# Front of batch b+2 interleaved with the back part of batch b, first jobs inside direction 3, convolution as diagonal matmuls

## Chip, cores and metric

The kernel runs on one core of a Trainium2 chip. The metric is the device time of one execution in microseconds (us), as the median of several; before the change it is 11132.13 us. The engines are called PE (TensorE), ACT (ScalarE), DVE (VectorE), POOL (GpSimd) and SP (SyncE, which issues all the DMAs here).

## What is computed

The input x is 8 batches of 96 channels on a 48 by 48 image (2304 positions). Two residual blocks follow each other, each behind a group norm (32 groups of 3 channels):

```python
x = x + L0(group_norm(x))        # Mamba-like 2D scan
x = x + L1(group_norm(x))        # channel attention over positions
# L0: 96 -> 2 x 192 channels (xx, z)
xx = gelu(conv3x3_depthwise(xx) + conv_b)            # 192 channels
# four directions k: rows, columns, and both backwards
dts, B, C = split(x_proj[k] @ xs[k])                 # 12, 16, 16 rows
delta = softplus(dt_w[k] @ dts + dt_b[k])            # 192 x 2304
h = h * exp(delta * A) + (delta * u) * B             # 192 channels x 16 states, over 2304 positions
y = sum_n(h * C) + u * D                             # directions summed
out = out_proj @ (layernorm(y) * gelu(z))
# L1: qkv = depthwise conv3x3(w_qkv @ x); 8 heads of 12; q, k normalised
out = w_proj @ softmax(q k^T * scale) v              # 2304 x 2304 scores a head
```

## The kernel before

Each batch passes three parts. The **front** is the group norm, the in-projection, the convolution, the x-projection and the nine first jobs of direction 0. The **directions** are the scans. The **back** is LayerNorm, the gate, the out-projection, the second group norm, the qkv projection and convolution, the norms of q and k, and their splitting in three bf16 parts each. The attention of batch b needs the back of b, and runs inside the directions of batch b+1; that of batch 7 runs alone at the end. `batches` writes this order for every engine: front(0), directions(0), back(0), then a loop over batches 1 to 7 of front, directions (with the attention of the batch before) and back, then attention(7).

**Directions.** There are four, each with 72 steps, written as three *stretches* of 24 steps (`BODY`); the first stretch is written out and the other two are turns of a loop. A step handles 8 channels x 16 states (128 partitions) and 768 positions. PE broadcasts delta*u by a bf16 matmul (`broadcast_u`, L1187 and L1188, in two PSUM slots), DVE multiplies it by B (`mult_b`, L992) and scans (L1013), ACT has taken the exponential of delta*A (L786, ring of six loads, issued five steps ahead), POOL multiplies by C (L691), PE sums the 16 states (`sum_tile`, L1200, bank 6) and DVE takes the sums out (L1020, L1022). B and C lie in `rep`; its thirds for the next direction are loaded as the old ones come free (`load_rep`).

**Jobs.** What a direction needs (delta, and delta*u split in three bf16 parts) is made one direction earlier by three jobs a stretch: a matmul with `dt_proj` (`job`, L1229, L1234), ACT's abs, relu, exp and ln (`job_stage`), POOL's six operations (`job_split`), and SP's stores (`store_delta`, `store_job`). They start at the steps `JOB_START = (1, 6, 13)`. Direction 3 makes none. Direction 0's nine jobs are made in the front, with DVE in POOL's place. The inputs u and dts lie in SBUF for the whole batch.

**Attention** in a step is three score matmuls (L1278), three exponentials on ACT (L795) and the value matmuls (L1212). Scores and jobs share PSUM banks 0 and 1 in turn (`SCAN_RING = 2`); a matmul waits until ACT has read what stood in its bank two entries before. The leftovers of the chunk before come at steps 1 to 4 (copy, denominators, their ln and exp, division), 7 (projection) and 16 (residual).

**The front's convolution** of 128 channels is DVE's (L977, nine operations over 2304 positions); that of 64 channels is ACT products and POOL sums (`front_units`). In the back, DVE convolves q and k (16 operations, L977) while ACT and POOL do v (`back_units`). All engines run their instructions in the order written.

## Time and profile before

| | us |
|---|---|
| median of 3 runs | 11132.13 (11129.79 to 11133.89) |
| profiled execution, its own time | 11130.08 |
| its span, first to last instruction | 11128.2 |
| busy: PE, DVE | 7464.3, 8043.1 |
| busy: ACT, POOL | 6426.9, 6356.7 |
| mean granted clock of PE | 0.786 |

The share of busy time is a mean over stages that differ. A granted clock of 1.0 is PE's 2.4 GHz, 0.5 is 1.2 GHz. A float32 matmul shows as two records. The numbers after L are lines of the kernel before. A row of the windows view has, in this order: the window's start and end and its width in us; busy us and instructions of PE, PE's weight loads, DVE, ACT and POOL; the granted clock; the DMA engines' busy share and their GB/s. A row of the lines view has the busy us of the group, the mean ns of one instruction, and the idle us before it with what ended it.

### The profile page before, as it was taken

To read this page: it belongs to the slowest core of one execution; us is meant where nothing else is said; L and a number is where in the kernel's file an instruction comes from. 1 tells how busy PE (TensorE), PEld (TensorE's weight loads), DVE (VectorE), ACT (ScalarE), POOL (GpSimd) and SP (SyncE) were. 2 spreads that over 40 slices of the span, in tenths; PEclk is the share of its full clock that TensorE was granted. 3 is DMA by queue.
4 is the path that set the end of the run, shared out by engine and by line. 5 is a ranking of instruction groups with operands and counts; after the bars stand their busy time and mean duration, and the time that the engine had idled before them with its cause. 6 is when DMAs were issued, how large, how long until landed. Compare 5 with 4: busy or idle time off the path is not lost.

```text
span 11128.2 us, 178500 instructions
## 1 busy us (share of the span) xinstructions
PE 7464.3 (67%) x53104; PEld 2416.6 (22%) x53104; DVE 8043.1 (72%) x6939; ACT 6426.9 (58%) x11827; POOL 6356.7 (57%) x4028
## 2 busy tenths in 40 slices
PE   3554468873688737885388844887458773688758
PEld 1221122221222212221122211222112221222212
DVE  4997668865788658886488955888568876788630
ACT  3332357753677437773377734776357753677468
POOL 3885447744677337774287733876348744577320
PEclk7555579975899758996599956999579985799779
DMA  3554145531555225551255513555135541555310
GB/s 89 182 183 141 24 144 179 176 109 35 162 180 173 83 53 168 183 171 57 75 175 183 170 32 101 179 183 161 31 118 180 180 130 25 151 181 174 102 23 19
DMA packets 686737, 1409.74 MB, mean 127 GB/s; under 512 B 74401, under 2 KB 334273, under 8 KB 678081
## 3 DMA queue, kind: packets, MB, share of 16 engines
q1 hardware_dynamic: 686016, 1401.21, 41.4%
q8 instruction: 322, 5.28, 0.2%
q14 instruction: 399, 3.26, 0.1%
HBM read 1186.22 MB, written 214.70 MB: 126 GB/s over the span
## 4 chain that ended last, share of the span: by engine, by line
PE 31%; issue 30%; DVE 10%; ACT 9%; DMA 9%; POOL 7%; SPq 3%; ACTq 1%; DVEq 0%; POOLq 0%
PE ps L1278 6%; PE ps L1212 6%; PE ps L1200 4%; ACT probs_buf L795 4%; POOL hc_buf L691 4%; PE ps L1357 3%; DVE ps L992 2%; PE ps L1387 2%; PE ps L1388 2%; DMA rep<-bc_scratch 2%; DVE job_buf L1013 2%; DVE rings L1013 2%; DMA rings<-delta_scratch 2%; PE ps L1187 1%; DMA delta_scratch<-job_buf 1%
## 5 line engine op out<-in xcount | busy, mean ns | idle before, releaser
L795 ACT ACTIVATE probs_buf<-ps 128x384 f32<-128x384 f32 x6912 | 3134.6, 492 | 1558.0 <-PE ps L1278 1508.7
L691 POOL TENSOR_TENSOR hc_buf<-rings,rep 128x768 f32<-128x768 f32 x1152 | 2094.1, 1818 | 2002.3 <-DVE rings L1013 1993.9
L1278 PE MATMUL ps<-qp_buf,kp_buf 108*128 108x384 bf16 (+1 forms) x6912 | 2222.5, 344 | 523.6 <-ACT probs_buf L795 230.3
L992 DVE TENSOR_TENSOR ps<-ps,rep 128x768 f32<-128x768 f32 x2304 | 2174.2, 944 | 476.2 <-PE ps L1188 302.3
L691 POOL TENSOR_TENSOR hc_buf<-job_buf,rep 128x768 f32<-128x768 f32 x1152 | 2092.2, 1816 | 706.0 <-DVE job_buf L1013 685.3
L1212 PE MATMUL ps<-probs_buf,v_buf 128*13 128x384 f32 x13824 | 1528.3, 516 | 31.8 <-ACT probs_buf L795 18.1
L1200 PE MATMUL ps<-hc_buf,sum_states 128*32 128x144 f32 x24576 | 1458.0, 324 | 131.8 <-POOL hc_buf L691 131.8
L1187 PE MATMUL ps<-st_buf,pick_channel 96*128 96x512 bf16 x2304 | 981.1, 426 | 768.9 <-DVE rings L1013 275.4
L1013 DVE TENSOR_TENSOR_SCAN job_buf<-rings,ps 128x768 f32<-128x768 f32 x768 | 1370.0, 1784 | 70.4 <-ACT rings L786 14.1
L1278 PEld LDWEIGHTS ps<-qp_buf,kp_buf 108*128 108x128 bf16 x6912 | 653.8, 97 | 2779.5 <-ACT probs_buf L795 1703.0
L786 ACT ACTIVATE st_buf<-st_buf,a_cols 128x768 f32<-128x768 f32 x1152 | 1072.5, 931 | 295.1 <-DMA st_buf<-delta_scratch 291.4
L786 ACT ACTIVATE rings<-rings,a_cols 128x768 f32<-128x768 f32 x1152 | 1068.8, 928 | 233.1 <-DMA rings<-delta_scratch 232.6
L1013 DVE TENSOR_TENSOR_SCAN rings<-st_buf,job_buf,ps 128x768 f32<-128x768 f32 x384 | 696.5, 1814 | 90.4 <-ACT st_buf L786 51.1
L1200 PEld LDWEIGHTS ps<-hc_buf,sum_states 128*32 128x32 f32 x24576 | 562.0, 117 | 918.1 <-issue 877.0
L1013 DVE TENSOR_TENSOR_SCAN job_buf<-st_buf,rings,ps 128x768 f32<-128x768 f32 x384 | 695.9, 1812 | 82.0 <-ACT st_buf L786 48.7
L1013 DVE TENSOR_TENSOR_SCAN rings<-rings,job_buf,ps 128x768 f32<-128x768 f32 x384 | 696.5, 1814 | 63.4 <-ACT rings L786 18.6
L298 POOL TENSOR_TENSOR rep<-rep,job_buf 96x1152 f32<-96x1152 f32 x128 | 618.7, 4867 | 202.3 <-ACT job_buf L286 202.3
L1188 PE MATMUL ps<-st_buf,pick_channel 96*128 96x256 bf16 x2304 | 684.9, 297 | 0.0
L1013 DVE TENSOR_TENSOR_SCAN rings<-st_buf,ps 128x768 f32<-128x768 f32 x384 | 673.3, 1753 | 4.0 <-issue 0.3
L1437 PE MATMUL ps<-rings,head_ones 96*96 96x384 f32 x192 | 101.7, 699 | 682.6 <-ACT rings L918 682.6
L311 DVE TENSOR_TENSOR job_buf<-job_buf 128x384 f32<-128x384 f32 x72 | 39.9, 554 | 599.8 <-ACT job_buf L771 599.8
L1187 PEld LDWEIGHTS ps<-st_buf,pick_channel 96*128 96x128 bf16 x2304 | 228.3, 99 | 1114.9 <-DVE rings L1013 429.5
(159 smaller groups left out, 8346.6 us busy)
## 6 DMA issues: line engine op xcount, KB each, us to landing
st_buf<-delta_scratch SPq DMA_DIRECT2D x1152, 384.0 KB
rings<-delta_scratch SPq DMA_DIRECT2D x1152, 384.0 KB
part_scratch<-job_buf SPq DMA_DIRECT2D x1152, 72.0 KB, 2.0
st_buf<-part_scratch SPq DMA_DIRECT2D x192, 432.0 KB, 7.5
rep<-bc_scratch SPq DMA_DIRECT2D x192, 384.0 KB
delta_scratch<-job_buf SPq DMA_DIRECT2D x192, 192.0 KB, 2.7
qp_buf<-qk_scratch SPq DMA_DIRECT2D x864, 36.0 KB
kp_buf<-qk_scratch SPq DMA_DIRECT2D x432, 72.0 KB
```

What stands on the lines that cost most here:

```text
L298: pool.tensor_tensor(dst, dst, tmp[i % 3], ALU.add).then_inc(s["tap_added"], 1)
L691: pool.tensor_tensor(hc[tile % 2][:, chunk(kk, v)], h_ring[t % 2], rep_third(1, kk, v), ALU.mult).then_inc(s["hc_ready"], 1)
L786: act.activation(da_ring[t % RD], da_ring[t % RD], ACT.Exp, scale=a_cols[:, bass.ds(q * (2 * TG) + (k * NG * TG + t // SPT), 1)])\
L795: act.activation(probs[(m % 2) * HG + h], bank(slots["score", p]), ACT.Exp, scale=SCALE)\
L992: dve.tensor_tensor(u_slot(t), u_slot(t), rep_third(0, kk, t % SPT), ALU.mult)\
L1013: dve.tensor_tensor_scan(o, d0, d1, init, ALU.mult, ALU.add).then_inc(s["h_ready"], 1)
L1187: pe.matmul(u_slot(t, 0, 512), pick(t), src[:, 0:512], start=True, stop=True)
L1188: pe.matmul(u_slot(t, 512, SC), pick(t), src[:, 512:SC], start=True, stop=True).then_inc(s["ubc"], 1)
L1200: ins = pe.matmul(ps[32 * j:32 * j + 32, BANK_Y, 0:YP], sum_states[:, 32 * i:32 * i + 32], hc[T % 2][:, col:col + YP], start=(i == 0), sto ...
L1212: ins = pe.matmul(ps[32 * h:32 * h + 13, BANK_PV, 0:PC], v_cols[:, m * HEADS + hg * HG + h, :], probs[(m % 2) * HG + h], start=(m == 0), s ...
L1278: pe.matmul(bank(slots["score", p]), k_parts[:, h, m * 128:(m + 1) * 128], q_ring[:, bass.ds(q, 1), h, :].rearrange("p s l -> p (s l)"), s ...
L1357: ins = pe.matmul(square(bank(2 * (c % 2) + odd)), w, x, start=(t == 0), stop=(t == 1))
```

## The change

- **Front.** The front of a batch is cut in 9 parts `f` of 24 steps: f=0 is the group norm, f=1 to 6 are one chunk of 8 image rows each, f=7 and 8 are the x-projection of the transposed image, three pieces each. A chunk is projected with one row of halo on either side (480 columns), copied to a padded buffer, convolved by nine matmuls with diagonal weights for 128 channels and nine for 64, passed through Gelu, stored, projected. All of this uses one PSUM bank and one set of buffers. Results go to DRAM (`u_scratch`, `xd_scratch`, `xn_scratch`, one place for each batch).
- **Where it runs.** Front 0 runs alone in `start`, front 1 inside the first nine stretches of batch 0's directions (one part a stretch, bank 1), front b+2 in the back of b, for b from 0 to 5 (bank 6): f=0 to 2 ahead of LayerNorm, f=3 to 6 beside the qkv convolution, f=7 in the norms of q and k, f=8 behind them. POOL does the normalising and the transposing copies.
- **Jobs.** Direction 3 of batches 0 to 6 makes the first jobs of the next batch. A job's inputs are loaded from DRAM (`load_job`, steps 0, 5, 11) and not kept in SBUF, the jobs start at (4, 9, 15), and ACT's and POOL's stages lie closer. The dt weights have 12 rows in place of 128; the third job's two halves go to two column halves.
- **Between.** `enter(b)` stores the q and k parts of b-1, loads B and C, the first deltas and states, and only then the queries and keys; these loads were issued during the front. In the back u is loaded again. The gate's matmuls use banks 2 to 5 and wait for LayerNorm's last logarithm.
- **Loops.** All three stretches are written out, each in a loop of one turn; batches 0, 6 and 7 are written out beside the loop over 1 to 5.
- At a direction's end the second state load goes ahead of the last two thirds of B and C. The last job of a stretch is stored in the next one.

```diff
 LN_EXP_TABLES = "natural_log_exp_and_others"
-DVE_CHAIN, ACT_CHAIN = 47, 2
...
+FRONT = K * NS - NS
+CHUNKS = NPC
+XC = PC + 2 * W
+FRONT_UNITS = ((0, 3, 0, 10), (1, 3, 10, 15), (3, 3, 15, 24),
+               (4, 4, 0, 10), (5, 4, 10, 15), (8, 4, 15, 24),
+               (9, 5, 0, 10), (10, 5, 10, 15), (13, 5, 15, 24),
+               (14, 6, 0, 10), (15, 6, 10, 15))
+FRONT_SUMS = (4, 9, 14)
...
-JOB_START = (1, 6, 13)
-ACT_STAGES = {"abs": 0, "relu": 0, "exp": 1, "ln": 2}
-POOL_STAGES = {"add": 4, "times_u": 5, "u0": 6, "u_rest": 7, "u1": 8, "u2": 9}
+LOAD_JOB = (0, 5, 11)
+JOB_START = (4, 9, 15)
+ACT_STAGES = {"abs": 0, "relu": 0, "exp": 1, "ln": 1}
+POOL_STAGES = {"add": 3, "times_u": 4, "u0": 5, "u_rest": 6, "u1": 7, "u2": 8}
...
-    ring = SCAN_RING if scan else RING
+    ring = (SCAN_RING if att else 1) if scan else RING
...
+        def front_bank(fb):
+
+            return 1 if isinstance(fb, int) and fb == 1 else BANK_Y
...
-        def batches(engine, front, directions, back, attention):
-
-            front(0)
-            directions(0, None)
-            back(0)
-            if NB > 1:
-                with engine.Fori(1, NB) as b:
-                    front(b)
-                    directions(b, b - 1)
-                    back(b)
+        def batches(engine, start, enter, directions, back, attention):
+
+            start()
+            enter(0)
+            directions(0, None, True)
+            back(0, 2)
+            with engine.Fori(1, NB - 2) as b:
+                enter(b)
+                directions(b, b - 1, True)
+                back(b, b + 2)
+            enter(NB - 2)
+            directions(NB - 2, NB - 3, True)
+            back(NB - 2, None)
+            enter(NB - 1)
+            directions(NB - 1, NB - 2, False)
+            back(NB - 1, None)
             attention(NB - 1)
 
         def stretches(engine, body):
 
-            body(0, True)
-            with engine.Fori(1, NS) as q:
-                body(q, False)
+            for q in range(NS):
+                with engine.Fori(0, 1):
+                    body(q, q == 0)
 
...
+            def load_job(b, kidx, k, q, j):
+
+                BI = kidx * NS + q
+                if j < 2:
+                    at_least(sp, "job_pool", (BI - 1) * NP + place(POOL_JOBS, 2, "times_u"))
+                else:
+                    sp.wait_ge(s["job_pool"], BI * NP + place(POOL_JOBS, 0, "times_u"))
+                    apart(sp)
+                    sp.wait_ge(s["dt_mm"], BI * JOBS + 2)
+                apart(sp)
+                u_src, d_src = of_batch(u_dram, b)[0, k % 2], of_batch(xd_dram, b)[0, k % 2]
+                r = DT_ROWS[k]
+                if j < 2:
+                    cols = piece(2 * q + j)
+                    sp.dma_start(job_d[:, piece(j)], d_src[r:r + R, cols]).then_inc(job_loaded[j], 16)
+                    sp.dma_start(job_u[:, piece(j)], u_src[0:DA, cols]).then_inc(job_loaded[j], 16)
+                else:
+                    for hf in range(2):
+                        cols = slice(hf * HL + q * PC, hf * HL + (q + 1) * PC)
+                        sp.dma_start(job_d[:, piece(hf)], d_src[r:r + R, cols]).then_inc(job_loaded[j], 16)
+                        sp.dma_start(job_u[64 * hf:64 * hf + 64, 0:PC], u_src[DA:DI, cols])\
+                          .then_inc(job_loaded[j], 16)
...
+                elif f <= CHUNKS:
+                    c, n = f - 1, fb * CHUNKS + f - 1
+                    if t == 1 and c == 0:
+                        sp.wait_ge(s["f_xn"], (fb + 1) * 16)
+                        apart(sp)
+                        load_chunk(fb, 0)
+                    if t == 21 and c + 1 < CHUNKS:
+                        load_chunk(fb, c + 1)
+                    if t == 20:
+                        sp.wait_ge(s["f_gelu"], 2 * n + 2)
+                        apart(sp)
+                        dst = of_batch(u_dram, fb)[0, 0]
+                        sp.dma_start(dst[0:DA, piece(c)], uc[0][:, :]).then_inc(s["f_us"], 16)
+                        sp.dma_start(dst[DA:DI, piece(c)], uc[1][:, :]).then_inc(s["f_us"], 16)
+                    if t == 23:
+                        sp.wait_ge(s["f_xd"], fb * 12 + c + 1)
+                        apart(sp)
+                        sp.dma_start(of_batch(xd_dram, fb)[0, 0, :, piece(c)], xd_stage[:, :])\
+                          .then_inc(s["f_xds"], 16)
...
+            def load_chunk(fb, c):
+
+                at_least(sp, "f_in", 2 * (fb * CHUNKS + c))
+                apart(sp)
+                lo, hi = chunk_rows(c)
+                src = of_batch(xn_dram, fb)[0, :, (8 * c - 1 + lo) * W:(8 * c - 1 + hi) * W]
+                sp.dma_start(xc[:, lo * W:hi * W], src).then_inc(s["f_chunk"], 16)
...
-                elif prep:
+                elif same:
+                    sp.wait_ge(s["ubc"], (kidx + 1) * DSTEPS)
+                    load_st(kk + 1, 1)
                     for c in range(1, SPT):
 
                         sp.wait_ge(s["hc_ready"], (kidx + 1) * DSTEPS - (SPT - c))
-                        load_rep(kk + 1, c)
-                    sp.wait_ge(s["ubc"], (kidx + 1) * DSTEPS)
-                    apart(sp)
-                    sp.wait_ge(part_stored[0], (kidx + 2) * NS * 128)
-                    load_st(kk + 1, 1)
+                        load_rep(b, kk + 1, c)
...
+            def start():
+                for f in range(FRONT):
+                    for t in range(BODY):
+                        front_step(0, f, t)
+                front_stored(0)
+                for q in range(NS):
+                    for j in range(JOBS):
+                        load_job(0, 0, KS_ORDER[0], q, j)
+                        store_delta(0, 0, q, j)
+                        store_job(0, 0, q, j)
+
+            def enter(b):
                 later = not (isinstance(b, int) and b == 0)
...
+                if later:
+                    sp.wait_ge(s["a_stored"], b * 96)
+                    apart(sp)
+                    first_queries_keys()
...
+            def back(b, fb):
+                if fb is not None:
+                    front_step(fb, 0, 0)
...
+                sp.dma_start(xn, of_batch(xn_dram, b)[0]).then_inc(s["xn_loaded"], 16)
+                if fb is not None:
+                    front_step(fb, 0, 19)
+                    for f in range(1, FRONT):
+                        for t in range(BODY):
+                            front_step(fb, f, t)
...
+                if fb is not None:
+                    front_steps(fb, 0)
+                    front_steps(fb, 1)
+                    front_steps(fb, 2)
...
+                if 1 <= f <= CHUNKS:
+                    c, n = f - 1, fb * CHUNKS + f - 1
+                    if t in (5, 7):
+                        i = (t - 5) // 2
+                        act.wait_ge(s["f_in"], 2 * n + i + 1)
+                        apart(act)
+                        if i == 0:
+                            at_least(act, "f_conv", 2 * n)
+                            apart(act)
+                        p = (128, 64)[i]
+                        dst = pads[i][:, :].rearrange("p (h w) -> p h w", w=PADW)[:, :, 1:1 + W]
+                        act.copy(dst, square(ps[0:p, front_bank(fb), 0:XC])).then_inc(s["f_pad"], 1)
+                    if t == 13:
+                        act.wait_ge(s["f_conv"], 2 * n + 1)
+                        apart(act)
+                        at_least(act, "f_us", 32 * n)
+                        apart(act)
+                        at_least(act, "f_ut", 2 * n)
+                        apart(act)
+                        act.copy(uc[0][:, :], bank(front_bank(fb))).then_inc(s["f_pre"], 1)
+                    if t == 19:
+                        act.wait_ge(s["f_conv"], 2 * n + 2)
+                        apart(act)
+                        act.wait_ge(s["f_pre"], n + 1)
+                        apart(act)
+                        act.activation(uc[1][:, :], bank(front_bank(fb), 64), ACT.Gelu, bias=conv_bias[1][0:64, :])\
+                            .then_inc(s["f_gelu"], 1)
+                        act.activation(uc[0][:, :], uc[0][:, :], ACT.Gelu, bias=conv_bias[0][:, :])\
+                            .then_inc(s["f_gelu"], 1)
+                        act.preload_act_table_set(LN_EXP_TABLES)
+                    if t == 22:
+                        project_out(fb, c)
+                if 2 <= f <= CHUNKS + 1 and t == 2:
+                    c, n = f - 2, fb * CHUNKS + f - 2
...
+            def back(b, fb):
+
+                if fb is not None:
+                    for f in range(3):
+                        front_steps(fb, f)
...
+                unit_products(act, b, back_units(), fb, front_steps)
+                if fb is not None:
+                    front_steps(fb, 6, 15, 24)
+                    front_steps(fb, 7, 0, 3)
...
+                if fb is not None:
+                    front_steps(fb, 8)
...
+                elif f <= CHUNKS:
+                    c, n = f - 1, fb * CHUNKS + f - 1
+                    if t == 4:
+                        pe.wait_ge(s["f_chunk"], (n + 1) * 16)
+                        if c in (0, CHUNKS - 1):
+                            pe.wait_ge(s["f_edge"], fb * 2 + (1 if c == 0 else 2))
+                        if c == 0:
+                            pe.wait_ge(s["f_std"], (fb + 1) * 2)
+                        else:
+                            pe.wait_ge(s["f_xd"], fb * 12 + c)
+                        pe.matmul(bank(front_bank(fb), n=XC), in_proj[:, 0:DA], xc[:, :], start=True, stop=True)\
+                          .then_inc(s["f_in"], 1)
+                    if t == 6:
+                        pe.wait_ge(s["f_pad"], 2 * n + 1)
+                        pe.matmul(bank(front_bank(fb), 64, XC), in_proj[:, DA:DI], xc[:, :], start=True, stop=True)\
+                          .then_inc(s["f_in"], 1)
+                    if 8 <= t < 13:
+                        if t == 8:
+                            pe.wait_ge(s["f_pad"], 2 * n + 2)
+                        conv_taps(fb, 0, 2 * (t - 8))
+                    if 14 <= t < 19:
+                        if t == 14:
+                            pe.wait_ge(s["f_pre"], n + 1)
+                            apart(pe)
+                        conv_taps(fb, 1, 2 * (t - 14))
+                    if t == 21:
+                        pe.wait_ge(s["f_gelu"], 2 * n + 2)
+                        pe.matmul(bank(front_bank(fb)), x_proj[0][:, 0:128], uc[0][:, :], start=True, stop=False)
+                        pe.matmul(bank(front_bank(fb)), x_proj[1][0:64, 0:128], uc[1][:, :], start=False, stop=True)\
+                          .then_inc(s["f_xp"], 1)
+                else:
+                    for i in range(3):
+                        if t == 6 + 6 * i:
+                            c = 3 * (f - CHUNKS - 1) + i
...
+            def conv_taps(fb, i, tap0):
+
+                p = (128, 64)[i]
+                for tap in range(tap0, min(tap0 + 2, 9)):
+                    ins = pe.matmul(square(bank(front_bank(fb), p)), conv_w[i][:, tap * p:(tap + 1) * p],
+                                    window(pads[i][:, :], tap, 8), start=(tap == 0), stop=(tap == 8))
+                    if tap == 8:
+                        ins.then_inc(s["f_conv"], 1)
...
+            def back(b, fb):
+
+                if fb is not None:
+                    for f in range(3):
+                        front_steps(fb, f)
                 pe.wait_ge(s["y_summed"], b + 1)
...
+                if fb is not None:
+                    for f in range(3, 7):
+                        front_steps(fb, f)
...
+                    if fb is not None and n:
+                        front_steps(fb, 7, 6 * n, 6 * n + 6)
+                if fb is not None:
+                    front_steps(fb, 8)
```

## Rows read from the trace of the kernel before

**Rows 1.** Windows: scans of batch 0, two gaps between scans, scans of batch 2
```profile
215.00:1056.00 841.00, 477.28 (x3718) 173.09 (x3716) 778.62 (x672) 308.90 (x394) 644.78 (x450) 0.53 0.54 173
...
1051.60:1500.50 448.90, 184.67 (x313) 63.94 (x314) 216.86 (x186) 131.23 (x183) 127.28 (x30) 0.52 0.20 52
2383.00:2844.00 461.00, 186.27 (x325) 63.69 (x326) 219.99 (x188) 132.71 (x186) 128.59 (x32) 0.53 0.20 53
2844.00:3731.80 887.80, 732.75 (x6314) 232.92 (x6312) 786.74 (x682) 671.21 (x1292) 666.20 (x471) 0.95 0.55 171
```

**Rows 2.** The page: granted clock of PE in 40 slices, in tenths
```profile
PEclk7555579975899758996599956999579985799779
```

**Rows 3.** Chain of waits, 2380 to 2850: start us, us, what ended last
```profile
2396.44 4.59 DMA out<-xres
...
2403.98 15.18 DMA hc_buf<-y_scratch
...
2431.40 1.65 PE ps L1387 x2
2433.05 1.58 PE ps L1388 x2
...
2513.70 14.93 PE ps L1429 x36
...
2603.45 4.97 DVE rep L977
...
2638.84 2.56 DVE st_buf L1148
...
2830.77 12.21 DMA st_buf<-part_scratch
```

**Rows 4.** Windows: LayerNorm to gate, end of qkv, beside that job, after it
```profile
1093.00:1168.00 75.00, 74.27 (x96) 21.20 (x96) 27.53 (x55) 19.67 (x35) 4.63 (x3) 0.50 0.00 0
...
1182.00:1190.00 8.00, 8.00 (x26) 3.92 (x24) 0.00 (x0) 4.94 (x12) 0.00 (x0) 1.00 0.00 0
...
248.00:254.00 6.00, 5.04 (x24) 2.21 (x24) 5.87 (x6) 1.84 (x4) 6.00 (x6) 0.54 0.53 146
254.00:257.00 3.00, 1.13 (x18) 0.52 (x18) 2.87 (x4) 2.51 (x5) 3.00 (x4) 0.98 0.73 214
```

**Rows 5.** Timeline of PE: a job in batch 0's scans, the qkv matmuls
```profile
249.27 2.77 PE L1234 MATMUL ps<-dts,dt_proj_b 128*128 128x384 f32 x4
...
1175.03 15.23 PE L1429 MATMUL ps<-job_buf,qkv_w 96*96 96x384 f32 x36 [2.05 <-DVE job_buf L965]
```

**Rows 6.** Lines of the whole span: a copy to the pad, a table load
```profile
L826 ACT COPY hc_buf<-ps 128x384 f32<-128x384 f32 x48 | 23.1, 481 | 135.8 <-PE ps L1341 130.7 <-POOL rings L655 5.1
...
L898 ACT ACT_TABLE_LOAD x8 | 10.3, 1283 | 0.1
```

**Rows 7.** Timeline of DVE in the first front: start us, us, what
```profile
141.22 0.56 DVE L311 TENSOR_TENSOR job_buf<-job_buf 128x384 f32<-128x384 f32 x1 [54.18 <-ACT job_buf L771]
...
194.56 0.56 DVE L339 TENSOR_TENSOR job_buf<-job_buf 128x384 bf16<-128x384 f32 x1
215.09 0.97 DVE L992 TENSOR_TENSOR ps<-ps,rep 128x768 f32<-128x768 f32 x1 [19.98 <-PE ps L1188]
```

**Rows 8.** The page: DMA issues, KB each, median us to landing
```profile
part_scratch<-job_buf SPq DMA_DIRECT2D x1152, 72.0 KB, 2.0
```

**Rows 9.** Windows: middle stretches with jobs (batches 2, 5) and without (batch 2)
```profile
3138.40:3213.20 74.80, 63.35 (x533) 19.89 (x532) 65.68 (x58) 57.21 (x111) 59.35 (x45) 0.93 0.59 182
...
7179.20:7249.40 70.20, 59.30 (x533) 19.31 (x532) 65.48 (x59) 56.98 (x111) 59.44 (x45) 1.00 0.58 194
...
3597.20:3664.60 67.40, 58.66 (x525) 17.93 (x524) 65.09 (x58) 52.66 (x99) 45.61 (x26) 0.97 0.53 168
```

**Rows 10.** Windows in batch 2: three steps from job 1, from job 2
```profile
3156.30:3170.90 14.60, 12.78 (x83) 3.24 (x75) 8.35 (x8) 8.17 (x17) 7.97 (x6) 0.70 0.55 165
3182.20:3190.90 8.70, 7.79 (x67) 2.86 (x67) 8.15 (x8) 6.47 (x14) 8.28 (x8) 1.00 0.70 209
```

628 lines of the change are left out of this document (381 added, 247 removed).

## The prediction

> **What bounds the kernel now.** I first cut the span into stages: the window view over the edges "end of the last scan of a batch" and "first multiplication of the next" [rows 1]. Batch 0's four directions take 841 us, with DVE busy 779 of them; the same directions with the previous batch's attention take 888 us, DVE busy 787. Between the scans lie 449 us once (batch 0 to 1) and about 461 us (batch 1 to 2 is shown, the five after it are alike), with DVE busy 220 and PE busy 186. So the scans are near DVE's pace and the stretches between them are chains in which engines hand over. The PEclk line says the same: high in the attention batches, 5 in the gaps and in batch 0 [rows 2].
>
> The chain of waits through one gap gives its parts [rows 3]: last scan ends 2383.0, output stored, y loaded by 2419.2, LayerNorm's first matmul at 2431.4 (48.4 us in); from there to the end of the qkv matmuls (2528.6) 97.2 us, set by PE; qkv convolution to 2608.4, 79.8 us, set by DVE; norms, splits and v columns about 37 us more (last subtraction ends 2641.2). That makes 262. The other 199 us are the next batch's front, its nine first jobs and the first loads. The change takes those 199 away and pays elsewhere.
>
> **A chunk of the new front.** Its steps depend on each other and share one PSUM bank: in-projection of 480 columns twice, a copy to the pad after each, 9 taps at 128 channels, a copy, 9 taps at 64, table load and two Gelus, two x-projection matmuls, a copy; only then the next chunk's first matmul. A float32 matmul with 384 columns and 128 weight columns takes 1.58 us from one to the next in the LayerNorm stream [rows 3]; its clock stays at 0.50, the 1.2 GHz level, though PE is busy 74.3 of 75 us [rows 4]. The 128-channel taps have that very shape: 9 x 1.58 = 14.2 us. The 64-channel taps are nearer to the qkv matmuls (96 by 96): their 36 records take 15.2 us, the last 8 us of it at 1.00, the 2.4 GHz level [rows 4, 5]; half as many records that start at 1.2 GHz: 9.3 us (bounds 5.8 and 13.3). In-projections 2.1 + 1.8; x-projection 2 x 1.58 plus drain 3.3; three copies and the last at 0.48 for 384 columns (L826), 0.57 for 480 [rows 6], 2.1; table load 1.28 [rows 6] and two Gelus, taken as copies, 1.0; twelve handovers 0.7. Sum 36 us a chunk. The tables that it needs back load under the x-projection.
>
> **The gap with a front in it** (after batches 0 to 5). PE and ACT run the norm and chunks 0 and 1 before they touch LayerNorm. x, y, u (new), the residual and xn are 8.5 MB on SP's one queue; y took 15.2 us for 4.1 MB [rows 3], so the queue is drained about 31 us after the loads begin (18 us in). The store of the normalised x is behind it (4.6 us, as the output's store), then the first chunk's load, about 3: ready at 56.5 us. Two chunks: 72. LayerNorm to qkv: 97.2 unchanged. Beside the qkv convolution lie chunks 2 to 5, 4 x 36 = 144 on PE and ACT, more than DVE's 79.8, plus 5 us (an ACT product first; chunk 5 waits for GpSimd's edge memset, which is queued behind a tap sum, taken as long as DVE's tap of 4.97 [rows 3]). The second x-projection, six pieces of about 4 us, is partly in the norms and wholly ahead of the splits: 37 + 24 = 61. Then entering the scans: rep, deltas, states and split q/k stores, 7.4 MB, about 35 us (the old last load took 12.2 at the end [rows 3]). Sum 56.5 + 72 + 97.2 + 149 + 61 + 35 = 471, against 461: +10, five times; the first gap starts 7 us earlier, 464 against 449: +15. Together **+65**. Bounds: a chunk of 30 or 42 us moves this by 216 either way.
>
> **The gap without one** (after batch 6): 262 + 9 for u's loads + 35 = 306 against 461: **-155**. After batch 7 only u's loads: **+9**.
>
> **The start.** Before, first jobs' splits begin at 141.2, end 195.1, first multiplication at 215.1 [rows 7]. Now nothing overlaps: x and norm 41, six chunks 216, second x-projection 28, nine jobs, 26 for the loads. A job took (195.1 - 141.2)/9 = 6 us pipelined; SP now runs load, store of delta and store of parts of one job before the next job's load, so its stages add up: load and landing 3.2 (a parts store lands in 2.0 [rows 8]), PE 1.6, ACT 2.2, DVE's six operations 3 (the last takes 0.56 [rows 7]), four issues 2, estimates all but the rows named: 12 each, 109. Sum 423: **+208**. Bounds 180 and 240.
>
> **Batch 0's directions** carry batch 1's front. DVE gets 5 us of statistics. PE has 477/288 = 1.6 us a step to do [rows 1] and about 2.8 to do it in; two cold taps add 3.15. At 1.2 GHz each of nine steps would run 4.75 us: with in- and x-projections +110 for all. But here a job's burst (2.77 us, L1234 at 249.27 [rows 5]) was followed by a stretch at 0.98 where 0.54 had been [rows 4], so PE streams mixed with the scan's do lift the clock. I take one to two slow steps per burst, 12 bursts, and a us here and there: **+45**. Bounds 5 and 115.
>
> **Directions with attention.** A middle stretch with jobs (direction 1) takes 74.8 us in batch 2 and 70.2 in batch 5, one without (direction 3) 67.4, DVE's pace: jobs cost 5 in the mean of the two [rows 9]. In batch 2's, the three steps from job 1 on (step 6, with the projection at step 7 and a ring of two banks) take 14.6 us, the three from job 2 on (step 13, alone) 8.7, against 8.4 at DVE's pace [rows 10]. The jobs now start at 4, 9 and 15, none beside the projection. I take 1.7 us a stretch in place of 5: eight stretches a batch, seven batches, with 80% of it granted: **-150**. Bounds 0 and -290. Direction 3 of batches 1 to 6 gets jobs: 18 x 1.7 = **+30** (bounds 10 and 95). All their issues count: SP gets eight more loads a stretch, landing some 3 us before a matmul four steps (11 us) later; the last job's parts are stored in the next direction, needed only there for the late groups. At direction boundaries the second state load now precedes two rep loads that DVE waits for: 24 x 0.4 = **+10**. One-turn loops: a change of stretch costs DVE nothing visible in the stretch without jobs (65.1 busy of 67.4 [rows 9]); taken as nothing, bound +-1 us each, 96 of them.
>
> Removed (DVE's and GpSimd's front convolution, ACT's products) is in the 199.
>
> **Sum:** +65 - 155 + 9 + 208 + 45 - 150 + 30 + 10 = +62. The profiled execution took 11130.1 us (span 11128.2), the median of three is 11132.1, so: 11190 us.
>
> **Rivals.** (1) Forecast, slightly slower, own range 11060 to 11400: 0.55.
> (2) The diagonal matmuls lift the clock in the gaps and at the start too. For: qkv matmuls and jobs did so within 7 us. Against: the LayerNorm stream, same shape as the 128-channel taps, 75 us busy, never did [rows 4]. It would take 6.5 off the big burst, the rest off the others, 13 us a chunk x 42 chunks = -546: 10640, faster. It decides from about 3 us a chunk. 0.12.
> [...]
> (3) Jobs cost in any place what they cost now: no -150, and 54 more in direction 3: 11190 + 204 = 11394, say 11400. For: bursts also dip the clock (0.93 against 0.97). Against: the job at step 13. 0.16.
> (4) Spacing frees the whole excess (-140 - 30) and batch 0 stays at DVE's pace (-45): 11190 - 215 = 10975, faster. For: POOL has the same jobs in batch 0 at full pace. 0.17.
> That the front does not leave the gap is part of 1: it is the point where PE and ACT run it in order.
>
> **Numbers.** 0.2% (22 us) is what a measurement here can tell. Above 11154: 0.40 of 1 and all of 3, 0.56; within: 0.07; below 11110: 0.08 of 1, 2 and 4, 0.37. Range 10930 to 11440: it leaves out 2 and the outer part of 3 (18 in 100) and holds 4.
>
> **What would show it.** First multiplication at about 423; batch 0's scans about 886 long; gaps of about 465 to 471 for the first six and 306 for the seventh; taps of L-lines with 128 columns 1.58 us apart at 0.50; LayerNorm's first matmul 128 us after the last scan; DVE idle beside chunks 2 to 5; middle stretches with attention near 69 us in all four directions. Wrong if a chunk takes under 32 us, if the first loads wait longer than 35, or if job stretches stay at 72 or more.

## The result, and the profile after

The changed kernel takes 11365.19 us, median of four runs (11252.58 to 11406.83), against 11131.96 for the kernel before in the same comparison (four runs, 11129.79 to 11133.89). The ratio of the means is 1.0194, 95% interval 1.0119 to 1.0268: slower, and whether by more or by less than 2% the interval leaves open. Its own runs differ by 1.4%, those of before by 0.04%. The profiled execution took 11346.75 us (span 11344.6, mean granted clock 0.778).

The windows view of the changed kernel, over the same stages as [rows 1]: the start, batch 0's scans, gap 0, batch 1's scans, gap 1, batch 2's scans, and the gap after batch 6, which has no front.

```profile
0.00:395.80 395.80, 181.40 (x319) 66.92 (x320) 30.59 (x68) 67.63 (x108) 17.28 (x23) 0.63 0.21 59
395.80:1293.10 897.30, 625.56 (x4002) 218.49 (x4000) 787.00 (x681) 354.96 (x489) 696.89 (x519) 0.57 0.57 184
1293.10:1707.00 413.90, 258.35 (x504) 97.34 (x504) 130.79 (x121) 113.83 (x153) 81.48 (x38) 0.61 0.22 64
1707.00:2644.10 937.10, 782.97 (x6338) 236.72 (x6338) 790.08 (x682) 688.52 (x1328) 703.73 (x524) 0.88 0.57 175
2644.10:3058.70 414.60, 250.56 (x516) 95.26 (x516) 136.50 (x122) 115.38 (x156) 88.77 (x40) 0.64 0.23 67
3058.70:3988.80 930.10, 761.60 (x6338) 235.02 (x6338) 788.76 (x682) 688.03 (x1328) 703.43 (x524) 0.90 0.58 177
9440.90:9750.00 309.10, 113.78 (x224) 39.73 (x224) 147.97 (x112) 76.38 (x94) 88.47 (x23) 0.54 0.22 61
```

A gap with a front fell from 461 to 414 although PE works 64 us longer in it; the scans with attention rose by 42 although DVE works only 2 us longer. Batch 2's scans have a granted clock of 0.90 where [rows 1] have 0.95. With the edges read off the first and last DVE instruction of each batch's scans, the whole span adds up:

| stage | before | after | change | forecast |
|---|---|---|---|---|
| start, to the first multiplication | 215.1 | 395.8 | +181 | +208 |
| batch 0's scans | 836.5 | 897.4 | +61 | +45 |
| six gaps with a front | 2751.7 | 2523.4 | -228 | +65 |
| gap after batch 6 | 456.4 | 309.1 | -147 | -155 |
| scans of batches 1 to 7 | 6181.9 | 6526.9 | +345 | -110 |
| last scan to the end | 686.7 | 692.1 | +5 | +9 |
| sum | | | +216 | +62 |

So two terms were wrong, in opposite directions, and each by more than the whole result. The timeline of PE in gap 1 shows the first: one chunk of the new front (start us, us, line, count).

```profile
2702.68 1.96 PE L1467 MATMUL ps<-xc,in_proj 96*128 96x480 f32 x2 [28.76 <-DMA xc<-xn_scratch]
2705.45 1.86 PE L1471 MATMUL ps<-xc,in_proj 96*64 96x480 f32 x2 [0.81 <-ACT pad_a L994]
2708.04 8.12 PE L1509 MATMUL ps<-pad_a,conv_w_a 128*128 128x384 f32 x18 [0.72 <-ACT pad_b L994]
2717.12 5.99 PE L1509 MATMUL ps<-pad_b,conv_w_b 64*64 64x384 f32 x18 [0.97 <-ACT uc_a L1002]
2725.79 1.63 PE L1484 MATMUL ps<-uc_a,x_proj_a 128*128 128x384 f32 x2 [2.68 <-ACT uc_a L1010]
2727.35 1.65 PE L1485 MATMUL ps<-uc_b,x_proj_b 64*128 64x384 f32 x2
2729.92 1.97 PE L1467 MATMUL ps<-xc,in_proj 96*128 96x480 f32 x2 [0.93 <-DMA xc<-xn_scratch]
```

The chunk's period is 27.2 us (2702.68 to 2729.92), not 36. The nine taps of 128 channels took 8.12 us, not 14.2, the nine of 64 channels 5.99, not 9.3: the clock did rise in them, to a mean of 0.74 over the first run and 1.00 over the second. Shortly behind, the LayerNorm, whose matmuls have the same 128 by 128 by 384 in every other place, still goes at 1.58 us each, and its 37.8 us are all busy at 0.50 (timeline, then the window over the whole LayerNorm).

```profile
2756.17 1.65 PE L1703 MATMUL ps<-st_buf,mean 128*128 128x384 f32 x2
2757.75 1.65 PE L1704 MATMUL ps<-st_buf,mean 64*128 64x384 f32 x2
```
```profile
2756.20:2794.00 37.80, 37.80 (x49) 11.96 (x48) 6.36 (x12) 9.31 (x18) 0.00 (x0) 0.50 0.02 7
```

The second wrong term is in the attention directions. Mean length of the three stretches of each direction, batches 1 to 6 (first / middle / last, us):

| | direction 0 | 1 | 2 | 3 | batch |
|---|---|---|---|---|---|
| before | 69.2 / 71.6 / 75.5 | 76.6 / 72.1 / 75.7 | 82.0 / 73.1 / 75.6 | 75.4 / 67.2 / 67.4 | 881.5 |
| after | 72.5 / 75.2 / 79.6 | 80.0 / 76.7 / 80.1 | 90.0 / 75.5 / 79.9 | 78.3 / 75.6 / 74.2 | 937.4 |

Middle stretches with jobs were to be about 69 in all directions. They are 75 to 77. The timeline of PE around the first job of a middle stretch (batch 2, direction 1, step 4, 5.7 us long):

```profile
3372.09 0.75 PE L1615 MATMUL ps<-qp_buf,kp_buf 108*128 108x384 bf16 x2
3374.22 1.52 PE L1566 MATMUL ps<-job_d,dt_proj_a 12*128 12x384 f32 x2 [1.38 <-ACT probs_buf L1060]
3375.68 1.48 PE L1549 MATMUL ps<-probs_buf,v_buf 128*13 128x384 f32 x8
3377.08 0.50 PE L1615 MATMUL ps<-qp_buf,kp_buf 108*128 108x384 bf16 x1
```

PE waits 1.38 us for ACT before the job's matmul, and from there on everything runs at half speed: the value matmuls take 1.48 us, where the same eight take 0.84 elsewhere. The 12-row matmul itself is new: the kernel before multiplied over all 128 rows of its padded operand [rows 5].

### The profile page after: what moved, and what is told of

It reads as the page before. It is cut to its first block, busy times and chain, and to the rows that moved or that the text cites. A ratio compares the mean times of both kernels' runs of the same rounds, so it can differ in the third digit from the quotient of the medians.

```text
span 11344.6 us, 176742 instructions
## 1 busy us (share of the span) xinstructions
PE 8357.5 (74%) x54832; PEld 2687.9 (24%) x54832; DVE 7439.6 (66%) x6473; ACT 6430.6 (57%) x11876; POOL 6332.1 (56%) x4464
## 4 chain that ended last, share of the span: by engine, by line
PE 42%; issue 16%; ACT 13%; DVE 12%; DMA 8%; SPq 4%; POOL 4%; ACTq 1%; DVEq 0%; POOLq 0%
PE ps L1549 8%; PE ps L1615 8%; PE ps L1509 6%; ACT probs_buf L1060 4%; PE ps L1537 4%; DVE rings L1281 4%; DVE ps L1260 3%; DMA rep<-xd_scratch 3%; DVE job_buf L1281 2%; ACT rings L1051 2%; PE ps L1703 2%; PE ps L1704 2%; DMA job_u<-u_scratch 2%; PE ps L1566 2%; PE ps L1524 1%
## 5 line engine op out<-in xcount | busy, mean ns | idle before, releaser
L1615 PE MATMUL ps<-qp_buf,kp_buf 108*128 108x384 bf16 x6912 | 2299.7, 357 | 623.0 <-ACT probs_buf L1060 274.8
L1537 PE MATMUL ps<-hc_buf,sum_states 128*32 128x144 f32 x24576 | 1530.5, 338 | 135.7 <-POOL hc_buf L880 135.7
L1549 PE MATMUL ps<-probs_buf,v_buf 128*13 128x384 f32 x13824 | 1606.1, 540 | 32.4 <-ACT probs_buf L1060 18.4
L1524 PE MATMUL ps<-st_buf,pick_channel 96*128 96x512 bf16 x2304 | 1009.2, 438 | 652.5 <-DMA qp_buf<-qk_scratch 287.6
L1281 DVE TENSOR_TENSOR_SCAN rings<-rings,job_buf,ps 128x768 f32<-128x768 f32 x384 | 696.3, 1813 | 157.7 <-ACT rings L1051 80.1
L328 POOL TENSOR_TENSOR rep<-rep,job_buf 96x1152 f32<-96x1152 f32 x128 | 490.2, 3848 | 435.4 <-ACT job_buf L312 435.4
L1509 PE MATMUL ps<-pad_b,conv_w_b 64*64 64x384 f32 x864 | 385.8, 605 | 50.6 <-ACT uc_a L1002 50.6
```

What stands on the lines that cost most here:

```text
L328: pool.tensor_tensor(dst, dst, tmp[i % 3], ALU.add).then_inc(s["tap_added"], 1)
L1281: dve.tensor_tensor_scan(o, d0, d1, init, ALU.mult, ALU.add).then_inc(s["h_ready"], 1)
L1509: ins = pe.matmul(square(bank(front_bank(fb), p)), conv_w[i][:, tap * p:(tap + 1) * p], window(pads[i][:, :], tap, 8), start=(tap == 0), s ...
L1524: pe.matmul(u_slot(t, 0, 512), pick(t), src[:, 0:512], start=True, stop=True)
L1537: ins = pe.matmul(ps[32 * j:32 * j + 32, BANK_Y, 0:YP], sum_states[:, 32 * i:32 * i + 32], hc[T % 2][:, col:col + YP], start=(i == 0), sto ...
L1549: ins = pe.matmul(ps[32 * h:32 * h + 13, BANK_PV, 0:PC], v_cols[:, m * HEADS + hg * HG + h, :], probs[(m % 2) * HG + h], start=(m == 0), s ...
```

## Experiments

Twelve kernels ran. Those numbered e1 to e4 each undo or try one thing on the changed kernel; the others combine such edits, or try them on the kernel before. Code is shown in part, with ... where lines are left out.

**e2_rows128: the job's matmul over 128 rows again**, rows 12 to 127 of both sides zero.

```diff
-        dt_proj = [sb("dt_proj_a", [R, K * DA]), sb("dt_proj_b", [R, K * DB])]
+        dt_proj = [sb("dt_proj_a", [128, K * DA]), sb("dt_proj_b", [128, K * DB])]
...
-        job_d = sb("job_d", [R, 2 * PC])
+        job_d = sb("job_d", [128, 2 * PC])
...
```

> The changed kernel with the job's step matmul over 128 rows again (its weights and its right side padded with zero rows), as the kernel before had it, in place of 12 rows. Theory B, that the 12-row matmuls lower TensorE's clock beside them (0.50 to 0.66 in the steps after a job): the steps from the job on get shorter, middle stretches fall from about 75.5 to 73 or less, batch 0's directions fall from 897 towards 880, the time by 100 to 200 us. Rival, that the rows of a matmul change nothing: all of it stays within 0.5 us a stretch, the time within 60 us of 11365.

Measured: 11177.08 us (11151.99 to 11203.82), 188 less than the change; ratio to before 1.0055 (1.0034 to 1.0076). A batch's scans fell from 937.4 to 909.0, middle stretches from 75.8 to 72.9 in the mean; batch 0's only from 897 to 892, where about 880 was expected. The timeline of PE in the same step of the same stretch:

```profile
3332.58 0.91 PE L1569 MATMUL ps<-job_d,dt_proj_a 128*128 128x384 f32 x2 [1.38 <-ACT probs_buf L1062]
3333.42 0.84 PE L1552 MATMUL ps<-probs_buf,v_buf 128*13 128x384 f32 x8
```

The wait is the same 1.38 us to the hundredth, but the clock stays up: 0.91 for the job, 0.84 for the values. The whole stretch in the windows view has a clock of 0.98, where the changed kernel's has 0.91 (second row, of that kernel):

```profile
3319.30:3391.40 72.10, 60.13 (x533) 19.10 (x532) 65.42 (x58) 57.54 (x111) 59.11 (x44) 0.98 0.61 199
```
```profile
3361.10:3436.10 75.00, 64.19 (x533) 19.60 (x532) 65.71 (x59) 57.60 (x111) 59.04 (x44) 0.91 0.59 191
```

More rows of zeros are faster here than few rows without. Theory B holds for the directions with attention; for batch 0's directions the fall of 5 us doesn't show it.

**e4_ln_same_rows: the LayerNorm's 64-row matmuls over 128 rows** (weights with zeros in the other half).

```diff
...
+                    pe.matmul(dst, mean192[:, :], x[0], start=True, stop=False)
+                    return pe.matmul(dst, mean_half[c // (NPC // 2)][:, :], x[1], start=False, stop=True)
...
-                        over_channels(bank(c % 2), (mean192[:, :], mean192), (y[0][:, piece(c)], y[1][part, cols]),
-                                      c).then_inc(s["ln_mean"], 1)
+                        mean_channels(bank(c % 2), (y[0][:, piece(c)], y[1][:, cols]), c).then_inc(s["ln_mean"], 1)
...
```

> The changed kernel with the layer norm's mean and variance matmuls of the 64-row half over all 128 rows (weights with zeros in the other half), so that all 48 of a batch have the same shape. Theory D, that a run of same-shape float32 matmuls lifts the clock and the turn from 128 to 64 rows keeps it down: the layer norm's records stand 0.64 us apart and then 0.32 at a granted clock of 1.00 in place of 0.79 at 0.50, its PE-bound stretch of 75 us falls to 45 or less, each gap falls by 25 to 40 us and the time by 200 to 320 us. Rival, that the clock follows the tables or the busy share alone (74.3 of 75 us busy at 0.50 in the kernel before): the spacing falls to 0.64 at most, the clock stays 0.50, and a gap falls by 10 to 15 us, the time by 80 to 120.

Measured: 11148.11 us (11104.69 to 11215.79), 217 less than the change; ratio to before 1.0025 (1.0008 to 1.0041). The six gaps with a front have a mean of 396.9 in place of 420.6. Timeline of PE, the LayerNorm's first matmuls, and the window over all of it:

```profile
2716.05 1.65 PE L1703 MATMUL ps<-st_buf,mean 128*128 128x384 f32 x2
2717.49 1.49 PE L1704 MATMUL ps<-st_buf,mean_lo 128*128 128x384 f32 x2
2718.77 1.36 PE L1703 MATMUL ps<-st_buf,mean 128*128 128x384 f32 x2
2719.97 0.81 PE L1704 MATMUL ps<-st_buf,mean_lo 128*128 128x384 f32 x2
```
```profile
2716.00:2736.00 20.00, 18.21 (x49) 9.66 (x48) 6.37 (x12) 9.56 (x19) 0.00 (x0) 0.90 0.05 17
```

From the second matmul to the third it is 1.28 us, and from the sixth on 0.65: 37.8 us became 19.5, although every second matmul now goes over 128 rows in place of 64. I had expected 75 to fall to 45; the 75 us of [rows 4] hold the gates and the output projection too, so only half of them had the edit. The gaps with a front are 24 us shorter in the mean, the last gap and the tail 21 each, less than the 25 to 40 expected. That the total still lies in the expected range (200 to 320) owes something to the spread of the runs: in the two profiles the gaps and the tail give 184 us, and 55 more stand in the scans of batches 1 to 7, which the edit doesn't touch. The same edit on the kernel before (e6_before_same_rows) gives the cleaner figure, 164.

**e8_taps_mixed: is it the shape, or the rows?** Every second tap of the 128-channel half as two matmuls of 128 rows and 64 columns.

```diff
...
                 for tap in range(tap0, min(tap0 + 2, 9)):
-                    ins = pe.matmul(square(bank(front_bank(fb), p)), conv_w[i][:, tap * p:(tap + 1) * p],
+                    for lo, n in ((0, 64), (64, 64)) if i == 0 and tap % 2 else ((0, p),):
+                        ins = pe.matmul(square(ps[lo:lo + n, front_bank(fb), 0:PC]),
...
```

> The changed kernel with every second tap of the 128-channel half of the convolution as two matmuls of 64 output channels, so that shapes alternate within the run: 13 matmuls in place of 9. Theory D: the run stays at 0.50 with a break before each, 13 x 2 x 0.79 is 20 us in place of 8 to 9, 11 us more in each of a front's six chunks, gaps rise from 415 to about 475, the time by 350 to 480 us. Rival, that the clock follows TensorE's busy share alone: the run warms up as before, 10 to 13 us, 2 to 4 us more a chunk, the time rises by 80 to 170 us.

Measured: 11406.70 us (11374.39 to 11429.76), 41 more than the change. My theory, in its form "any turn of shape", fell: the run warmed up as before (timeline of PE).

```profile
2704.24 9.17 PE L1510 MATMUL ps<-pad_a,conv_w_a 128*128 128x384 f32 x26 [0.72 <-ACT pad_b L994]
```

26 records in 9.17 us, against 18 in 8.12; over the 36 such runs in the gaps it is 9.69 against 8.19 in the mean. The starts of the records tell where that goes. The two halves of a divided tap start within 0.01 us of each other, so the extra matmuls as such cost nothing; the turn does. From one tap to the next it is 1.58 or 1.48 us while the clock is at 0.50, and 0.84 or 0.80 at 1.00, where undivided taps stand 1.28 and 0.65 apart. So a turn between 128 and 64 columns costs 0.2 to 0.3 us at the lower clock, as the LayerNorm's turn between 128 and 64 rows does (1.58 against 1.28), but the clock rises in spite of it, and in the LayerNorm it does not.

The run's gaps with a front are 16 us longer in the mean, more than six times 1.5 us. Every one of them also holds a long POOL sum, of the kind described at the end of the next section, and in the changed kernel's profile one gap does.

**e6_before_same_rows: the LayerNorm's edit alone, on the kernel before.**

> The kernel BEFORE with the layer norm's mean and variance matmuls all over 128 rows, nothing else. Theory D (same-shape runs of float32 matmuls reach the full clock whatever stands around them): its layer norm falls from 37.8 to about 19.5 us, the projections behind it gain a few us, 20 to 24 us in each of 8 back parts, time 11130 less 160 to 190: about 10955. Rival, that the gaps of the changed kernel are warm for another reason (its front's work ahead of the layer norm): here the clock stays 0.50, only the weight loads' breaks go, 37.8 to 31, and the time falls by 50 to 60 to 11075.

Measured: 10964.39 us (10961.07 to 10966.65); ratio to before 0.9853 (0.9836 to 0.9869). So the LayerNorm needs no front ahead of it to get warm. The timeline of PE at the LayerNorm's end shows the other side of it within 10 us:

```profile
1113.78 0.81 PE L1388 MATMUL ps<-rings,mean_hi 128*128 128x384 f32 x2
1114.42 0.81 PE L1418 MATMUL ps<-job_buf,in_proj 96*128 96x384 f32 x2
1115.16 0.86 PE L1419 MATMUL ps<-job_buf,in_proj 96*64 96x384 f32 x2
...
1120.75 1.59 PE L1393 MATMUL ps<-st_buf,out_proj_a 128*96 128x384 f32 x2 [3.09 <-DVE st_buf L1112]
1122.27 1.59 PE L1394 MATMUL ps<-st_buf,out_proj_b 64*96 64x384 f32 x2
1123.79 1.65 PE L1418 MATMUL ps<-job_buf,in_proj 96*128 96x384 f32 x2
```

The gates' matmuls behind the LayerNorm are warm; after a wait of 3.09 us the clock is down, and while the output projection turns between 128 and 64 rows it stays down. e12_before_all_rows below takes these turns away.

**e5_rows_both: both edits on the changed kernel.**

> The changed kernel with both edits that helped by themselves: the job's matmul over 128 rows (188 us less) and the layer norm's mean and variance matmuls all over 128 rows (217 us less). Theory: the clock's losses lie in different stretches (attention directions; gaps) and the two gains add up, so 11365 less 405 is 10960, 150 us under the kernel before. Rival: one warm stretch takes clock from the next and about a third is lost, 11090.

Measured: 10984.81 us (10905.87 to 10992.90), ratio 0.9875 (0.9858 to 0.9891). The gains add up (405 forecast, 380 measured).

**e1_places: the jobs at steps 5, 9 and 13.**

```diff
-LOAD_JOB = (0, 5, 11)
-JOB_START = (4, 9, 15)
+LOAD_JOB = (0, 5, 10)
+JOB_START = (5, 9, 13)
...
-POOL_STAGES = {"add": 3, "times_u": 4, "u0": 5, "u_rest": 6, "u1": 7, "u2": 8}
+POOL_STAGES = {"add": 2, "times_u": 3, "u0": 4, "u_rest": 5, "u1": 6, "u2": 7}
...
```

> The changed kernel with its three jobs of a stretch at steps 5, 9 and 13 in place of 4, 9 and 15 (steps in which no value matmuls fall), the GpSimd stages one step earlier and the load of the third job at step 10. Theory A, that a job costs most where its matmul shares a step with the value matmuls: step 4 (5.0 to 5.7 us now) falls to about 3.5, middle stretches of the attention directions fall from about 75.5 to 72 or less, 18 of them and the others alike, and the time falls by 150 to 250 us to about 11150. Rival, that a job costs what its ScalarE work and its clock cost, wherever it stands: step 5 takes over the 5.0 to 5.7 us of step 4, the middle stretches stay at 75 to 76 and the time stays within 60 us of 11365.

Measured: 11530.79 us (11511.59 to 11581.01), 166 more. The places cost more than that. This kernel also issues, in the start, the loads of a job ahead of the stores of the one before, and its first multiplication comes at 345.1 in place of 395.8, 51 us earlier; the scans of batches 1 to 7 take 236 us more. Step 7, the projection's, takes 5.7 us and step 14 takes 5.5; middle stretches 77.8. Sharing a step with value matmuls was not the cause; theory A fell. The timeline of PE shows how step 14 comes about:

```profile
3413.42 0.86 PE L1575 MATMUL ps<-job_d,dt_proj_b 12*64 12x384 f32 x4 [0.94 <-ACT probs_buf L1065]
...
3416.35 0.50 PE L1620 MATMUL ps<-qp_buf,kp_buf 108*128 108x384 bf16 x1 [1.09 <-ACT job_buf L969]
...
3417.85 1.48 PE L1554 MATMUL ps<-probs_buf,v_buf 128*13 128x384 f32 x8
```

In this step the job holds one of the two banks that the scores use. PE waits for a bank before the job (0.94), a score waits for ACT to have read the job's bank (1.09), and then the clock is down and PE is late for the broadcasts too.

**e3_ln_later: the job's logarithm one step later.**

```diff
-ACT_STAGES = {"abs": 0, "relu": 0, "exp": 1, "ln": 1}
+ACT_STAGES = {"abs": 0, "relu": 0, "exp": 1, "ln": 2}
```

> The changed kernel with the job's logarithm on ScalarE one step behind the exponential again (offset 2 in place of 1). Theory C, that two job operations in each of two steps running are more than ScalarE has room for: the steps 5, 10 and 16 fall by about 0.3 us each, the next ones rise by less, middle stretches fall by 1 to 2 us, the time by 50 to 150 us. Rival, that ScalarE waits for TensorE there and not for itself: nothing moves by more than 0.5 us a stretch, the time stays within 60 us of 11365.

Measured: 11379.01 us (11329.84 to 11402.66), the change's own time; middle stretches 75.4. Theory C fell.

**e7_before_places: the places alone, on the kernel before.**

```diff
-JOB_START = (1, 6, 13)
+JOB_START = (4, 9, 14)
...
```

> The kernel BEFORE with its three jobs of a stretch at steps 4, 9 and 14 in place of 1, 6 and 13 (the part store of the third one step earlier behind it), nothing else. My prediction's step: with the jobs further from the leftovers of the stretch before, the middle stretches of directions 0 to 2 fall from about 72 to 69.5 and the time falls by 80 to 150 us. Rival from the trace of the changed kernel: step 4 takes over (5 us there, its matmul waits 1.4 us for ScalarE before it and the scores after it wait for the job's bank), the middle stretches stay or rise to 72 to 74, the time rises by 0 to 100 us.

Measured: 11288.34 us (11280.76 to 11291.38), ratio 1.0143 (1.0126 to 1.0160): 160 us slower, more than the 100 that the rival gave it at most. Middle stretches with jobs went from 72.3 to 75.7, batch 0's scans from 836.5 to 865.7. The step of my prediction was wrong in its sign.

**e9_rows_places and e10_places_alone: the places of before in the changed kernel**, with and without the two row edits. The first job's operands are loaded at step 20 of the stretch before, but at step 0 in the first stretch of directions 0 and 3.

```diff
-LOAD_JOB = (0, 5, 11)
-JOB_START = (4, 9, 15)
+LOAD_JOB = (20, 1, 8)
+JOB_START = (1, 6, 13)
...
```

> The changed kernel with the three edits together: job matmul over 128 rows, layer norm over 128 rows (these two: 10985), and the jobs at steps 1, 6 and 13 with the ScalarE and GpSimd stages and the stores of the kernel before; the first job's operands are loaded at step 20 of the stretch before. Theory: the places 4, 9 and 14 cost the kernel before 158 us in three directions of seven batches (21 directions), so giving them back in the changed kernel, which has jobs in 27 directions there, gives 160 to 210 us more: about 10800, middle stretches with jobs at 71 to 72.5, fourth direction as the others. Rival: with the loads of the job's operands in SP's queue the place doesn't matter, 10985 within 60 us.

> The changed kernel with only the places, stages, loads and stores of the jobs as in the run before (12-row job matmuls and the layer norm as changed). Theory (place and rows add up): 11365 less 160 to 210, about 11180; middle stretches 73 to 74. Rival, that the 12-row matmuls make it the same at any place: 11300 or more.

Measured: 10990.39 us (10906.28 to 11026.84), the time of e5_rows_both, and 11437.06 us (11397.24 to 11486.55), 72 more than the change. Neither gave what e7_before_places promised. Stretches of e9_rows_places against e5_rows_both, mean of batches 1 to 6: middle 71.6 against 72.8, last 74.4 against 76.0, but the first ones of directions 0 and 3 are 77.2 and 87.1 against 70.2 and 76.3. There the load comes too late (timeline of PE, batch 2, direction 3):

```profile
3659.74 1.65 PE L1571 MATMUL ps<-job_d,dt_proj_a 128*128 128x384 f32 x2 [12.10 <-DMA job_u<-u_scratch]
```

Its two loads were issued at 3647.4 and 3647.9, behind the boundary's other issues. By these two profiles the places are worth some 15 us a batch, and the late loads take back 18. e10_places_alone against the changed kernel gives nearly the same, 12 and 18. A load in time for these two stretches wasn't tried.

**e11_all_same_rows and e12_before_all_rows: the output projection over 128 rows too**, in e9_rows_places and in e6_before_same_rows.

> The run with rows and places together, and the output projection's 64-row half over 128 rows as well (weights with zeros in the other half). Theory D: the stage of gates and output projections, 38 us a batch at 0.50 in the kernel before, has no turn from 128 to 64 rows any more and goes to 20 to 26 us: 80 to 120 us less, about 10700. Rival, that this stage waits for VectorE and ScalarE once the matmuls are fast: 40 us less.

> The kernel BEFORE with the layer norm and the output projection over 128 rows (the first alone gave 10964). Theory D: 80 to 120 us less than that, about 10865; with the run before this one it tells what the change itself is worth when both have warm matmuls: the changed kernel wins by 100 to 200 us if the jobs are back in their places. Rival: 40 us less.

Measured: 10975.43 us (10948.83 to 11028.02), ratio 0.9866 (0.9845 to 0.9888), and 10928.84 us (10924.58 to 10957.51), ratio 0.9829 (0.9814 to 0.9844). The second is 36 less than e6_before_same_rows, near the rival's 40; the first 15 less than e9_rows_places, which their intervals don't tell apart. But in the stage itself the trace of e12_before_all_rows shows what theory D says; PE waits for DVE for 2.26 us before the last of the projections, and hardly elsewhere. Behind the same wait of 3.09 us the matmuls soon go at half the pace, but then the clock comes back, and it stays up to the end of the projection, although the gates between still turn between 128 and 64 columns (timeline of PE):

```profile
1121.26 0.89 PE L1426 MATMUL ps<-st_buf,out_proj_a 128*96 128x384 f32 x2 [3.09 <-DVE st_buf L1112]
...
1125.77 1.59 PE L1426 MATMUL ps<-st_buf,out_proj_a 128*96 128x384 f32 x2
1127.16 1.48 PE L1428 MATMUL ps<-st_buf,out_lo 128*96 128x384 f32 x2
...
1130.34 0.89 PE L1426 MATMUL ps<-st_buf,out_proj_a 128*96 128x384 f32 x2
1131.06 0.81 PE L1428 MATMUL ps<-st_buf,out_lo 128*96 128x384 f32 x2
```

In the two profiles the seven gaps and the tail are 71 us shorter, nearer to theory D's 80 than to 40, and the scans of batches 1 to 7, which the edit doesn't touch, 27 us longer. e12_before_all_rows is the fastest kernel of the study by its median, and it does not contain the change. Its expectation had also said that the changed kernel would win by 100 to 200 us once both have these matmuls over 128 rows. It did not: 10975 against 10929 with all edits, and 10985 (e5_rows_both) against 10964 (e6_before_same_rows) with the LayerNorm's, in the second pair with ratios to before whose intervals overlap. What the change takes out of the gaps it gives back in the start and in the scans (in the profiles of these last two 421 less in the gaps, 177 more in the start and 174 more in the scans).

## Why the prediction was right or wrong

"Slightly slower" was right, the size 175 us short (11190 forecast, 11365 measured, in the range), and the reasons were largely wrong: an error of -293 and one of +455 hid each other. That the time fell into the range, and on the side that was forecast, was luck.

**The gap with a front** (forecast +65, measured -228). The step that failed is the price of the taps, taken at the LayerNorm's 1.58 us because "the 128-channel taps have that very shape". They had; what sets the LayerNorm's pace is the matmul between them, of 64 rows. With the measured 8.1 and 6.0 the chunk's own sum is 26.6, and six of them take 471 to 414. Over all 36 chunks in the gaps the two runs take 8.2 and 7.1 in the mean; that gives 27.8 and a gap of about 422, and the mean of the six is 421. So the chunk's other terms stand, as a sum. This is rival 2, to which I gave 0.12, about two thirds of it in size (9 us a chunk, not 13). I had read the rows against it correctly and drawn the wrong rule from them. The Trainium skill, "TensorE: Matmul & The Clock Gate", section "Why this matters for your kernels", says to keep TensorE continuously busy to get to the full clock; the taps agree with it (1.00 over the second run), the LayerNorm before does not (74.3 us busy of 75 at 0.50 [rows 4]), and e4_ln_same_rows shows what to add here: rows that don't alternate.

**The attention directions** (forecast -150, +30 and +10, measured +345). By the runs there are four causes. They overlap, and their figures are not a sum:
- The 12-row matmuls: 178 us of it, from the sums of scans of batches 1 to 7 (6526.9, and 6349.3 in e2_rows128). The edit stands in the section on the change, but the prediction's sum has no term for it, and no reason why not: it priced how many matmuls and when, not their rows.
- The places: "the jobs now start at 4, 9 and 15, none beside the projection. I take 1.7 us a stretch in place of 5". In the kernel before the same kind of places cost 160 us more (e7_before_places). I had read 14.6 us behind job 1 and 8.7 behind job 2 [rows 10] as a matter of leftovers. What the steps of e1_places show is a ring of two banks, in which a job makes PE and ACT wait for each other. In the changed kernel the places cost some 12 to 15 us a batch. I have no run that says why it is less than there.
- Late operands. Direction 2's first stretch grew by 8.0 us. In the scans of batches 1 to 7 the trace has PE waiting 61 us in all for the job's operands from DRAM (19 waits, longest 7.3), 35 of them at the start of direction 2, 5 us each time; e9_rows_places shows the same wait where it is worse. The prediction counted the loads' issues and let them land "some 3 us" before use, which forgot what stands ahead of them in SP's queue at the start of direction 2 (nine key loads and 16 stores of y in batch 2, issued from 3516.0 to 3537.8, the job's loads at 3539.3 and 3539.9).
- Direction 3 has jobs where it had none: with 128 rows it takes 222.6 against 210.1, +12.5 a batch, 75 for six. The forecast had +30, with 95 as its bound.

Without the first of these, in e2_rows128, the scans of batches 1 to 7 are 167 us longer than before: in batches 1 to 6 75 for direction 3's jobs and 44 for direction 2's first stretch; 48 are left for everything else.

Rival 3 ("jobs cost in any place what they cost now", 11394; its 54 for direction 3 would be 59 at 3.3 us a stretch) gave nearly the median, but it did not have the clock. It is right for e2_rows128, where middle stretches with jobs take 72.9 against 72.3.

**The rest** held: first multiplication 396 (423, though the terms named for it add up to 420), batch 0's scans 897 (bounds 5 and 115 about +45), the gap without a front 309 (306), the tail +5 (+9). Batch 0's +61 need not all be the front's matmuls: the places alone gave +29 there in the kernel before. LayerNorm's first matmul comes 112 us behind the last scan in gap 1, not 128: two chunks of 27 us in place of 36 make the difference.

Why runs of the changed kernel differ by 1.4% is shown in part. Single gaps are some 20 to 35 us longer than most (gap 2 with 447.7), others in other runs. In the ten profiles of kernels with the new front one of POOL's sums of the qkv convolution takes 29 to 30 us in 22 of the 60 gaps, and in the other 38 none takes over 5.0. The 22 are the longest gaps of their profiles, and all six of e8_taps_mixed are among them. The copy by ACT that PE needs comes only after that sum, and PE's second run of taps, once it starts, goes at half the pace (timelines of POOL, PE and DVE in gap 2, and of DVE in gap 1):

```profile
4222.48 35.47 POOL L328 TENSOR_TENSOR rep<-rep,job_buf 96x1152 f32<-96x1152 f32 x3 [35.66 <-ACT job_buf L312]
```
```profile
4259.82 11.75 PE L1509 MATMUL ps<-pad_b,conv_w_b 64*64 64x384 f32 x18 [11.72 <-ACT uc_a L1002]
```
```profile
4235.09 2.61 DVE L1245 SCALAR_TENSOR_TENSOR probs_buf<-kp_buf,qkv_taps,probs_buf 96x2304 f32<-96x2304 f32 x1
...
2900.99 4.96 DVE L1245 SCALAR_TENSOR_TENSOR probs_buf<-kp_buf,qkv_taps,probs_buf 96x2304 f32<-96x2304 f32 x1
```

While that sum lasts, DVE's operations of the same convolution follow each other at 2.61 us; beside POOL sums of ordinary length, in gap 1, many take 4.96 or 4.97. That the number of such gaps makes the runs differ, and what decides whether one comes about, is not shown.

## What to carry over

Before you price a matmul stream from a row of the trace, look at what stands between its records: the same shape was twice as fast where its neighbours had the same number of rows. Padding a matmul with zero rows can be the cheaper form, and cutting them away, as this change did with the job, belongs in the sum as an edit. When a small stage is put into a stream, ask which bank or buffer it takes from the stream's own ring, and issue the loads of its operands early enough for the longest queue that can stand ahead of them at a boundary.
